# Folds from the decays' tile in the opening, weights split by column groups, own orders for the first and last scan

## The reference, cut to what matters

```python
# x: (8, 512, 256); d = 0 runs forwards over the tokens, d = 1 backwards
def mamba2(x, Win, convw, convb, dtb, Alog, Dsk, normw, Wout):
    z, xBC, dt = split(x @ Win, [512, 512 + 640])          # 256 -> 1160
    xBC = silu(causal_conv4(xBC) + convb)                  # 640 channels
    xs, B, C = split(xBC, [512, 576])                      # 8 heads of 64; 64 states
    dt = softplus(dt + dtb); dA = exp(-exp(Alog) * dt)
    h_t = dA_t * h_{t-1} + dt_t * B_t (x) x_t;  y_t = C_t . h_t
    y = (y + Dsk * xs) * silu(z)
    return (y * rsqrt(mean(y * y) + 1e-5) * normw) @ Wout
out = concat([mamba2(ln(x), forward), flip(mamba2(flip(ln(x)), backward))]) @ Wo + bo
x = x + out
x = x + ln(x) @ W.T + b + (ln(x) @ V_r) @ C.T
```

## Time and profile before

| | us |
|---|---|
| median of 3 runs | 652.66 (652.19 to 652.87) |
| the profiled execution, its own time | 651.56 |
| its span, first to last instruction | 649.7 |
| PE, ACT, DVE, POOL busy in it | 612.0, 535.0, 502.9, 363.4 |
| mean granted TensorE clock | 0.987 |

### The profile page before, as it was taken

One profiled execution on the slowest core, in us unless ns is written; L12 is line 12 of the kernel. 1 busy time (PEld: TensorE's weight loads), 2 busy tenths in 40 slices (PEclk: granted clock), 3 DMA queues, 4 the chain that ended last, 5 costly groups with the idle time before them and its releaser, 6 DMA issues.

```text
span 649.7 us, 13284 instructions
## 1 busy us (share of the span) xinstructions
PE 612.0 (94%) x3996; PEld 499.0 (77%) x3996; DVE 502.9 (77%) x1052; ACT 535.0 (82%) x1207; POOL 363.4 (56%) x367
## 2 busy tenths in 40 slices
PE   1778999999999999999999999999999999999896
PEld 1557778887888878888788878888788878888684
DVE  4638879796879869796878869697797969788463
ACT  4369997988979797988979798888979799897932
POOL 1004764866555855667646674657638664556813
PEclk9979999999999999999999999999999999999897
DMA  6424360608233360606325180514406070334400
GB/s 214 149 59 146 92 179 4 204 4 245 55 94 110 97 203 0 203 1 194 106 52 151 53 248 0 144 60 150 150 10 194 9 235 26 102 105 118 152 1 32
DMA packets 42920, 70.70 MB, mean 109 GB/s; under 512 B 7888, under 2 KB 30480, under 8 KB 42896
## 3 DMA queue, kind: packets, MB, share of 16 engines
q1 hardware_dynamic: 42896, 70.40, 35.9%
HBM read 59.37 MB, written 4.72 MB: 99 GB/s over the span
## 4 chain that ended last, share of the span: by engine, by line
PE 78%; ACT 6%; DVE 6%; issue 5%; POOL 5%; POOLq 0%; ACTq 0%; DVEq 0%
PE mi L571 17%; PE py L537 9%; PE pj L446 9%; PE pj L448 8%; PE pj L447 8%; PE py L549 7%; PE mi L524 4%; PE mi L626 4%; POOL yg L1706 3%; PE mi L504 2%; PE mi L557 2%; DVE xdt L1276 2%; PE mi L619 1%; DVE xc L1264 1%; ACT xs L868 1%
## 5 line engine op out<-in xcount | busy, mean ns | idle before, releaser
L1264 DVE SCALAR_TENSOR_TENSOR xc<-pj,cw,xc 128x510 f32<-128x510 f32 (+2 forms) x240 | 175.0, 740 | 18.4 <-ACT xc L859 16.2
L889 ACT ACTIVATE bs<-bs,s_all 128x128 f32<-128x128 f32 x512 | 158.8, 387 | 0.0
L1706 POOL TENSOR_TENSOR yg<-yg,sz 128x512 f32<-128x512 f32 x60 | 76.9, 1281 | 121.6 <-DVE yg L1313 121.6
L446 PE MATMUL pj<-xnt_hi,w_hi 128*128 128x512 f32 x288 | 121.8, 423 | 10.5 <-DVE xc L1264 4.0
L448 PE MATMUL pj<-xnt_hi,w_lo 128*128 128x512 f32 x288 | 114.7, 398 | 0.0
L447 PE MATMUL pj<-xnt_lo,w_hi 128*128 128x512 f32 x288 | 114.6, 398 | 0.0
L571 PE MATMUL mi<-wc,yg 128*128 128x256 f32 x480 | 112.2, 388 | 1.0 <-DVE hst L1305 1.0
L571 PEld LDWEIGHTS mi<-wc,yg 128*128 128x128 f32 x480 | 90.0, 192 | 16.9 <-issue 5.5
L1291 DVE TENSOR_TENSOR bs<-bs,gm 128x512 f32<-128x512 f32 x128 | 85.9, 677 | 1.4 <-ACT bs L895 0.6
L859 ACT ACTIVATE xc<-pj,cb,cw 128x512 f32<-128x512 f32 x80 | 61.3, 767 | 29.2 <-PE pj L448 28.6
L1683 POOL TENSOR_TENSOR xw<-xdt,w_end 128x512 f32<-128x512 f32 x48 | 49.1, 1044 | 55.1 <-ACT w_end L877 54.5
(11 more groups left out here) (150 smaller groups left out, 1023.1 us busy)
## 6 DMA issues: line engine op xcount, KB each, us to landing
bs<-rows_dram SPq DMA_DIRECT2D x64, 512.0 KB, 4.8
es<-rows_dram SPq DMA_DIRECT2D x128, 96.0 KB, 4.2
xin<-in_x SPq DMA_DIRECT2D x8, 512.0 KB, 5.2
cc<-bcm SPq DMA_DIRECT2D x32, 128.0 KB, 2.3
xres<-in_x SPq DMA_DIRECT2D x8, 512.0 KB, 3.8
out<-ot SPq DMA_DIRECT2D x32, 128.0 KB, 3.2
cz<-bcm SPq DMA_DIRECT2D x16, 128.0 KB, 2.4
rows_dram<-s_rows SPq DMA_DIRECT2D x128, 4.0 KB
```

Source lines behind the costliest of these rows:

```text
L446: pe.matmul(ps[:], hi(k), xnt_hi[:, k, :], start=(k == 0), stop=False)
L889: i = nc.scalar.activation(bs[:, h, Q * c:Q * c + Q], bs[:, h, Q * c:Q * c + Q], ACT.Relu, bias=s_all[:, d, 0, c, h:h + 1], scale=-1.0)
L1264: i = dve.scalar_tensor_tensor(xc[:, t, to], pj[bank][:, of], cw[:, d, t, KW - 1 - s:KW - s], xc[:, t, to], ALU.mult, ALU.add)
L1706: pool.tensor_tensor(yg[:, d, p, :], yg[:, d, p, :], sz[:, d, p, :], ALU.mult).then_inc(yg_ready, 1)
```

## The change

Four parts. (1) The raw inputs of the folds lie in `bs`, the tile of decays, which nothing else uses before the first scan, instead of in `yg`, `xres` and `ot`. All nine folds move from the first forward scan into the opening; the first `repeat_heads` waits for the last of them. (2) The raw weights are loaded and split in two column groups (640 columns of tiles 0 to 4, 512 of tiles 5 to 8), each with its own semaphore; x of batch 0 comes in four loads, one a chunk; the clearing memsets `zeros` go behind the first norm; the order of the first loads is new. (3) The opening, the first forward scan, the loop's two scans and the last reversed scan have lists of their own on each engine. (4) The loop's lists are ordered anew as well. The arithmetic is unchanged.

```diff
+WIN = [slice(DI, 2 * DI + 2 * NS), slice(0, DI)]
-START = (["a0", "a1", "dtm", "dtt", "0S", "0ST"]
-         + ["w0", "w1", "0bt", "0x0", "w2", "0x1", "0x2", "0x3", "w3", "0s0", "w4", "0s1", "0s2", "w5", "w6",
-     "1S", "1ST", "w7", "w8"])
-LOOP = ["1bt", "1x0", "1x1", "1x2", "1x3", "a0", "a1", "1s0", "1s1", "dtm", "dtt", "0ss", "0o0", "0o1",
-        "1s2", "0S", "0ST", "0bt", "0x0", "0x1", "0x2", "0x3", "0s0", "1ss", "0s1", "0s2", "1o0", "1o1",
+START = (["a0", "a1", "dtm", "dtt", "w0", "w1", "w2", "w3", "0S", "0ST", "w4", "w5", "w6", "w7", "w8"]
+         + ["0bt", "0x0", "0x1", "0x2", "0s0", "0x3", "1S", "1ST", "0s1", "0s2"])
+LOOP = ["1bt", "1x0", "1x1", "1x2", "1x3", "a0", "a1", "1s0", "1s1", "dtm", "dtt", "0ss", "0o0", "1s2",
+        "0o1", "0S", "0ST", "0bt", "0x0", "0x1", "0x2", "0s0", "0x3", "1ss", "0s1", "0s2", "1o0", "1o1",
...
-        raw_woutT = yg[:, 1]
-        raw_wo = xres[:]
-        raw_ffT = ot[:, 2:4, :]
+        raw_woutT = bs[:, 0:KI, :]
+        raw_wo = bs[:, KI:KI + 2, :].rearrange("p a (b n) -> p (a b) n", b=2)
+        raw_ffT = bs[:, KI + 2, :].rearrange("p (k n) -> p k n", k=KD)
...
+                if isinstance(b, int) and b == d == p == 0:
+                    for n in range(2 * KI + 1):
+                        bank, used = misc_use("start", 0, f"w{n}")
+                        sp.wait_ge(mi_full[bank], used + 1)
...
-            def split_high(d):
-                act.wait_ge(w_loaded[d], 16 * KD)
-                for k in range(KD):
-                    nc.scalar.activation(w_hi[:, d, k, :], raw_w[d][k], ACT.Copy).then_inc(w_hi_ready[d], 1)
+            def split_high(d, g, k):
+                act.wait_ge(w_loaded[d][g], 16 * KD)
+                nc.scalar.activation(w_hi[:, d, k, WIN[g]], raw_w[d][k][:, WIN[g]], ACT.Copy).then_inc(w_hi_ready[d][g], 1)
```

The DVE list of the opening, between `soft_abs` and `soft_one` (before: `soft_one` directly behind `soft_abs`):

```diff
                 soft_abs("start", 0)
+                conv(0, 0, 2, 1)
+                split_low(0, 1, 1)
+                conv(0, 0, 1, 3)
                 soft_one(0)
```

ACT's list of the loop's reversed scan, new (its first two thirds):

```diff
+                b_tokens(phase, it, 1)
+                bound(b, 1, 0)
+                gate(b, 1, NT - 1)
+                decay_w(b, 1)
+                decay_e(b, 1)
+                norm_high(phase, it, 0)
+                norm_high(phase, it, 1)
+                decay(b, 1, 0)
+                bound(b, 1, 1)
+                bound(b, 1, 2)
+                bound(b, 1, 3)
+                square(phase, it, b, 0, 3)
+                conv_start(nxt, 0, 0)
+                decay(b, 1, 1)
+                dt_bias(phase, it)
+                decay(b, 1, 2)
+                conv_start(nxt, 0, 1)
+                soft_exp(nxt)
+                bound(b, 1, 4)
+                decay(b, 1, 3)
+                bound(b, 1, 5)
+                decay(b, 1, 4)
+                decay(b, 1, 5)
+                soft_log(nxt)
+                conv_start(nxt, 0, 2)
+                bound(b, 1, 6)
+                conv_end(nxt, 0, 0)
+                bound(b, 1, 7)
+                decay(b, 1, 6)
+                decay(b, 1, 7)
```

More of the change, by code:

```diff
@@ L651, in reversed_scan @@
                 mix(phase, it, b, 0, 1)
+                state(phase, it, b, 1, 2)
+                intra(b, 1, 0)
+                intra(b, 1, 1)
                 mix(phase, it, b, 0, 2)
+                mix(phase, it, b, 0, 3)
+                inter(phase, it, b, 1, 0)
+                sums(phase, it, nxt, 0)
+                inter(phase, it, b, 1, 1)
+                project(nxt, 0, 3)
+                project(nxt, 0, 4)
+                intra(b, 1, 2)
+                s_transposed(phase, it, nxt, 0)
@@ L690, in forward_scan @@
                 x_tokens(phase, it, b, 0, 0)
-                if not more:
-                    fold(2)
                 scores(phase, it, b, 0)
@@ new lines, in reversed_scan @@
+                bound(b, 1, 6)
[3 more added lines that the diff above has]
+                decay(b, 1, 7)
+                conv_start(nxt, 0, 3)
+                square(phase, it, b, 1, 0)
+                conv_start(nxt, 0, 4)
+                row_copy(phase, it, 0)
+                square(phase, it, b, 1, 1)
+                row_decays(phase, it, 0)
+                conv_end(nxt, 0, 1)
+                gate(nxt, 0, 5)
+                conv_end(nxt, 0, 2)
@@ new lines, in reversed_scan @@
+                squares(phase, it, 0)
+                soft_du(nxt)
+                soft_dd(nxt)
+                conv(nxt, 0, 0, 3)
+                soft_rq(nxt)
+                weights(phase, it, b, 1, 3)
+                conv(nxt, 0, 1, 1)
+                mix(phase, it, b, 0, 0)
+                mix(phase, it, b, 0, 1)
+                state(phase, it, b, 1, 2)
+                weights(phase, it, b, 1, 4)
+                conv(nxt, 0, 1, 2)
+                soft_ratio(nxt)
+                conv(nxt, 0, 2, 1)
@@ L1420, in reversed_scan, with last_scan @@
+            def last_scan():
+                phase, it, b = "last", 0, NB - 1
+                x_tokens(phase, it, 1, 0)
+                x_tokens(phase, it, 1, 1)
+                x_tokens(phase, it, 1, 2)
+                scores(b, 1)
+                x_tokens(phase, it, 1, 3)
+                state(phase, it, b, 1, 0)
+                squares(phase, it, 0)
+                weights(phase, it, b, 1, 0)
                 weights(phase, it, b, 1, 1)
+                state(phase, it, b, 1, 1)
+                mix(phase, it, b, 0, 0)
+                mix(phase, it, b, 0, 1)
@@ L1524, in forward_scan @@
                 if ahead:
                     norm1_aggr(b + 1, 2)
-                if more:
-                    mix(phase, it, last, 1, 3)
+                norm2_aggr(last, 0)
+                norm2_aggr(last, 1)
+                norm2_aggr(last, 2)
+                norm2_aggr(last, 3)
+                weights(phase, it, b, 0, 5)
+                conv(b, 1, 2, 1)
                 if ahead:
```

1159 lines of the change are left out of this document (663 added, 496 removed).

## The result

The changed kernel took **635.62 us** in the median of 4 runs (635.01 to 636.39), the kernel before 652.42 us (652.01 to 652.87) on the same chip: a ratio of 0.9753 with a 95% interval from 0.9736 to 0.9770. On another chip, in the set of the last experiments, the unchanged file took 635.36 us (ratio 0.9734, 0.9711 to 0.9758). The profiled execution took 635.01 us and has a span of 633.2 us, 16.5 less than before.

What follows compares the result with a forecast made beforehand. PE was taken to bound the turns, ACT's list the opening and first scan. 6.8 (opening and first scan) + 0 (turns) + 4.4 (last scan) = 11.2 us off 652.66 gave 641.5 us; 8-in-10 range 635 to 649.

Steps and rivals of the forecast that it cites:

- Bounds: Whole kernel: turns bound by PE; opening and first scan limited by ACT's list, with 9.43 us of holes.
- Start of the chain: Opening: earlier x and weights and reordered steps start the first logarithm 1.6 us earlier, between 0 and 2.5.
- ACT's list: Logarithm to first turn: 44.4 us of ACT work plus remaining holes, 47.0 instead of 52.2, so 5.2 us less.
- such small waits: Logarithm to first turn: ACT holes still left after the change, 2.6 us kept of 9.43.
- Turns: Seven turns: PE's work and waits stay, 0 us gained; a turn stays at 74.5 us.
- delicate place: PE's wait for al at `sums` in each turn: slack falls from 2.6 to 0.1 us.
- seventh load: One more ACT table load in each turn, 1.30 us, hidden by ACT's 9.2 free us a turn.
- Last scan: Last scan: sooner mixes and a clock that stays up, 4.4 us taken of 4.8; bounds 1.0 and 5.5.
- the sooner mixes: Start of the last scan: with `decay_w` as ACT's first step, PE's mixes start at 607.4, 3.1 us sooner.
- the clock: Last scan: if the shorter hole keeps PE's clock up, the first 24 mix matmuls win another 1.7 us.
- Rivals: Turns give back idle time, 0.12; opening's holes only move, 0.12; softplus bounds turns, 0.07; small new turn waits, 0.09.
- (a): Seven turns: they give back their idle time as well, 5.0 us, for 636.5 us; chance 0.12.

Runs made afterwards that it cites:

- late folds: Changed kernel with the nine folds moved from the opening back into the first scan, their inputs in the old tiles: 644.24 us, ratio 0.9889.
- filled kernels: Changed kernel with 26 identity transposes filling PE's waits in the opening: 634.48 us; with 24 more behind the last mix: 632.61 us.
- turns as before: Changed kernel with the seven turns' lists and bank order put back to the old ones: 637.77 us, ratio 0.9782.
- last scan, ACT order: Changed kernel with ACT's last scan beginning in its old order and PE transposing the B tile first: 638.80 us, ratio 0.9791.

## Why the prediction was right, and where it was off

- *Bounds.* Right for the turns. For the opening and first scan the prediction said "I read ACT's list as the limit there, with 9.43 us of holes in it". After the change that is so (43.99 of 44.72 us). Before it, it was half the truth: in the first scan PE was busy for 32.57 of 34.38 us and ACT for 31.29. The view by one long stretch (43.46 and 42.77 of 52.20) hid that PE was full in its second part (32.57 of 34.38) and idle for much of its first (10.88 of 17.81 busy).
- *Start of the chain.* Forecast 1.6 us, between 0 and 2.5; the logarithm came 2.77 us sooner (24.87 for 27.64). The first projection was forecast at 14.05 and came at 14.35. Much of the rest is PE's rate, which doubled at 17.05 us in this execution and at 20.65 in the one before; in the kernel with ACT's old last order, whose opening is the same, it doubled at 20.48 and the logarithm came at 26.58. In the seven executions with this opening the logarithm comes at 24.87 to 26.84 us, 25.8 in the mean; in the two with the old one at 27.34 and 27.64. So 1.6 was a fair term, and the profiled execution a lucky one.
- *ACT's list.* Its work was forecast as 44.4 us and measured as 43.99. The holes were **the mis-sized term**: "For such small waits I keep 2.6 us" stood there, and 0.73 were left. The run with late folds shows why for the first scan: its holes were waits for a PE that had folds in it and for banks that folds held, 4.0 us of them, and with the folds gone 0.06 us are left (28.55 of 28.61). Such a step must be priced on PE as well as on ACT, and taking the folds out is worth 6.4 us in the first scan alone. Together the stretch is 44.7 us where 47.0 was forecast, and the opening with first scan 10.2 us shorter where 6.8 was, just outside the bounds of 2 to 10. By the medians it is 9.8.
- *Turns.* Forecast 0; between 0.6 and 2.3 us were won, and not from PE's idle time, which grew from 5.0 to 6.85 us: PE's own work, which the prediction did not reckon to change, became about 2 us shorter. The delicate place was right: al was ready at 241.23 + 0.18 = 241.41, PE came to `sums` at 241.84, so 0.4 us of slack where 0.1 was forecast and 2.6 had been. The seventh load is hidden, as forecast, as far as the runs show. Where the prediction costed it, a switch took 1.30 us; here the load at 242.23 and the activation at 243.52 give 1.29. The 2.66 us that the Trainium skill has for it (ScalarE: Activation LUTs, What ACT_TABLE_LOAD costs) are not what this trace shows. What was not seen: that with an early SiLU SP's list can copy C first, and must not without it (19 us).
- *Last scan.* Forecast 3.1 us for the sooner mixes; they are 2.6 behind the first projection, 3.0 with the B tile put alike. Forecast 1.7 for the clock; 16 mixes in 3.72 us are 5.6 for 24, so 1.5. In all 4.4 were forecast and 5.0 came. A further 0.8 us lies behind the start of the last mixes, 14.9 us before the end instead of 15.7. There the prediction had nothing ("norm, feed and stores in their old order"), but the lists of DVE and POOL in the tail are new. Whether they won anything the runs can't tell: with them that piece took 14.6 to 15.9 us in eleven executions, with the old lists 15.0 and 15.7.
- *Rivals.* None of the four occurred. (a) came nearest in time, but its mechanism didn't: PE's idle time in the turns was not given back.

The sum missed by 5.6 us: 3.4 in opening and first scan, 1.3 in the turns and 0.6 in the last scan by the traces, and the rest between the medians and the profiled executions. All three errors have one sign. So 635.62 us lies outside the 637 to 646 that the prediction gave its own forecast, nearest to the 636.5 of (a), whose mechanism did not occur; that it lies in the wide range from 635 to 649 is in part luck. What was right is the largest term's mechanism: the folds go out of the scan into holes of ACT's list that nothing else filled.

## What to carry to other kernels

Cut a stretch where the kind of work changes before naming its limit: over 52 us PE and ACT were both busy for some 43, as if each had room, but in the last 34 us both were nearly full (32.57 and 31.29) and all the room was in the first 18. A step that is moved must be priced on every engine it uses and with the banks it holds, not only on the engine that was read as the limit. And before one line of a tuned set of lists is moved, look in the other lists for the line that was put where it is because of it: here a copy in SP's queue turned a nearly harmless reordering into some 20 us.

## What was not expected of the hardware

The same opening took 41.2 to 43.2 us in different executions. Two things move it, both ahead of the logarithm, for from the logarithm to the opening's end all seven took 16.4 us. One is the start of PE's first transposes, which stand behind the norm of x; DVE waited 0.8 to 1.0 us in all for the loads of x in the executions with the early starts, and 1.4 to 1.8 in the three others. The second is the moment at which PE's matmuls of the first projections change from 0.43 to 0.23 us apart. For the seven kernels that share the opening:

```
rate doubles at us    17.05  17.83  18.60  18.32  19.14  20.48  20.80
first transposes at    9.51   9.45  10.21   9.51   9.48  10.08  10.33
from these to rate     7.54   8.38   8.39   8.81   9.66  10.40  10.47
opening, us           41.24  41.52  42.27  41.82  42.16  42.97  43.22
opening less start    31.73  32.07  32.06  32.31  32.68  32.89  32.89
```

Counted from the first transposes, the opening's length goes with the moment of the change: up to 1.2 us of the spread are the clock's and up to 0.9 the start's. The page's clock column does not show the change. In the kernel after it reads 1.00 for the slow stretch as well:

```profile
9.50:17.05 7.55, 4.64 (x15) 3.70 (x16) 5.18 (x9) 3.17 (x7) 0.00 (x0) 1.00 0.96 307
```

Later in a program the column does show it. In the kernel with late folds the matmuls from 34.12 us on are 0.43 us apart again, and it reads 0.50:

```profile
34.12:38.12 4.00, 4.00 (x9) 3.13 (x10) 2.13 (x4) 3.96 (x8) 0.00 (x0) 0.50 0.45 123
```

That these are the two levels of the clock, 1.2 and 2.4 GHz, is read from the rates and from the filled kernels, where PE was at the fast rate from the second matmul of the first projection on (14.61 and 15.08 us) and the opening took 39.9 and 40.4 us, which is 30.5 us from the first transposes in both. At the start of a program the distance of like matmuls is the measure, not the column. The Trainium skill says that the moment of the rise varies from run to run (TensorE: Matmul & The Clock Gate, Part 1: The HAM clock gate); the traces agree, but the half microsecond either way that it gives for it there is less than what they show, 7.5 to 10.5 us after PE's first transposes.

A difference of 2 us between two kernels that start alike is therefore not yet one of the edit. Part of what the medians of `turns as before` and `last scan, ACT order` show may be this, since their stretches behind the opening show less.
